# A graph network on one core: leaner lists in the first stage, two scalar products merged, and the needs of the third pass's gathers found one aggregate sooner

## The reference, cut to what matters

```python
# first layer: three passes
for l in range(3):
    neigh = segment_sum(h[src], dst) * inv_deg
    h = h @ Ws_self[l] + neigh @ Ws_neigh[l] + bs[l]      # relu after passes 0 and 1
x = layernorm(x + h)
# second layer, called with idx_i = src, idx_j = dst: messages of an edge
s, v = hs[idx_j], hv[idx_j]                               # 32 scalars, 32 x 3 vectors
Wf = (ssp(f_ij @ W1 + b1) @ W2 + b2) * rcut               # filters, four kinds are used
s*ys*Wf0, (v.yv)/sqrt(3)*Wf1, s*yv*Wf2, v*ys*Wf3          # summed per source node
x = layernorm(x + dense(sums))
```

## Time and profile before

| | us |
|---|---|
| median of 3 runs (lowest, highest) | 1964.1 (1961.87, 1965.44) |
| the profiled execution | 1961.11 |
| its span, first to last instruction | 1959.3 |
| mean granted TensorE clock | 0.985 |
| PE busy | 1863.8 (95%) |
| DVE busy | 1285.2 (66%) |
| POOL busy | 1075.7 (55%) |
| ACT busy | 591.9 (30%) |

### The profile page before, as it was taken

The page is one execution under the profiler, slowest core; times in us unless marked ns, Lnnn a source line. Parts: engine busy times, 40 slices in busy tenths (PEclk is TensorE's granted clock), DMA queues, the critical chain, the costliest instruction groups (busy, mean ns, idle before and its releaser), DMA issues. The chain is left out here.

```text
span 1959.3 us, 23685 instructions
## 1 busy us (share of the span) xinstructions
PE 1863.8 (95%) x8451; PEld 1191.1 (61%) x8451; DVE 1285.2 (66%) x1989; ACT 591.9 (30%) x1380; POOL 1075.7 (55%) x1018
## 2 busy tenths in 40 slices
PE   6799989999999999999999999999998988999996
PEld 3344445555555555555555555666665877888885
DVE  5899999869973334333333434555553988999997
ACT  1355542300000000000000000111113876888884
POOL 4000000000038878888887886188887777777773
PEclk9899999999999999999999999999998998999998
DMA  5145454322223323332332234455554344444441
GB/s 151 60 167 173 154 205 169 126 90 88 84 86 107 112 82 112 113 95 92 95 99 80 90 95 142 141 187 192 192 192 152 96 103 108 108 108 111 112 116 50
DMA packets 127305, 236.72 MB, mean 121 GB/s; under 512 B 28134, under 2 KB 70835, under 8 KB 127184
## 3 DMA queue, kind: packets, MB, share of 16 engines
q1 hardware_dynamic: 93152, 179.50, 28.6%
q0 software_dynamic: 34032, 55.66, 10.6%
HBM read 159.94 MB, written 75.11 MB: 120 GB/s over the span
## 5 line engine op out<-in xcount | busy, mean ns | idle before, releaser
L1115 PE MATMUL low<-table,abuf 125*125 125x512 f16 x3750 | 843.1, 380 | 4.8 <-DVE abuf L1554 4.8
L1115 PEld LDWEIGHTS low<-table,abuf 125*125 125x125 bf16 x3750 | 505.0, 137 | 300.0 <-issue 27.5
L957 PE MATMUL mid<-wbuf,h_t 128*125 128x512 f32 x1200 | 558.9, 602 | 6.1 <-DVE st_out L1601 4.5
L820 POOL DMA_INDIRECT by_src<-scat_row,sort x416 | 482.4, 1160 | 126.0 <-issue 118.5
L825 POOL DMA_INDIRECT table<-msg_table,wbuf x294 | 318.5, 1083 | 90.7 <-issue 81.3
L957 PEld LDWEIGHTS mid<-wbuf,h_t 128*125 128x125 f32 x1200 | 214.8, 190 | 210.3 <-issue 199.6
L812 POOL TENSOR_TENSOR scat_row<-scat_row 128x64 f32<-128x64 f32 x26 | 16.0, 615 | 524.3 <-DVE sort L1721 523.8
L1608 DVE SCALAR_TENSOR_TENSOR y<-low,inv_deg,st_in 125x512 f32<-125x512 f32 x75 | 56.2, 750 | 315.5 <-PE low L1115 198.4
L1554 DVE TENSOR_TENSOR abuf<-abuf,row_scale 125x3125 bf16<-125x3125 bf16 (+3 forms) x84 | 256.5, 3059 | 2.1 <-DMA abuf<-adj 2.0
L1149 PE MATMUL low<-table,wbuf 128*125 128x256 f32 x900 | 217.2, 392 | 31.2 <-DVE table L1851 30.7
L850 POOL DMA_INDIRECT sort<-msg_table,sort x156 | 193.0, 1237 | 82.3 <-issue 82.0
(11 more groups left out here) (215 smaller groups left out, 1636.3 us busy)
## 6 DMA issues: line engine op xcount, KB each, us to landing
abuf<-adj SPq DMA_DIRECT2D x75, 781.2 KB, 4.9
adj<-table SPq DMA_DIRECT2D x25, 781.2 KB, 4.6
states<-st_out SPq DMA_DIRECT2D x75, 256.0 KB, 2.0
st_in<-states SPq DMA_DIRECT2D x75, 256.0 KB, 4.9
early_rows<-sort POOLq DMA_DIRECT2D x30, 320.0 KB, 2.8
table<-early_rows SPq DMA_DIRECT2D x25, 384.0 KB, 6.5
by_src<-scat_row,sort POOLq DMA_INDIRECT x416
by_src<-blank SPq DMA_DIRECT2D x25, 252.0 KB, 4.0
```

What stands on the lines that cost most here:

```text
L820: pool.indirect_dma_start(out=by_src, out_offset=bass.IndirectOffsetOnAxis(ap=place_i[:, k * PIECE + j:k * PIECE + j + 1], axis=0), in_=sc ...
L957: last = pe.matmul(to[0:TN, :], h_t[i % 2][:, k, :], weights[l % 2][:, a, k, :], start=k == 0, stop=k == KC - 1)
L1115: last = pe.matmul(p_agg[k % 2][0:TN, :], a_tile[k % 3][:, a, :], table[ps % 2][0:TN, a, h, :], start=a == 0 and h == 0, stop=a == TILES - ...
```

## The change

- **First stage.** The degrees are counted by POOL (5 compares of 640 elements, then sums by halves), no longer by L1467 and L1469 on DVE. The codes are transposed in two parts, and the number of rounds needs only the first. The store and the load of the degrees move from SP's w = 4 to w = 12 and 13, their transpose and reciprocals to w = 14. PE waits for the rounds behind product 5, not ahead of it. Columns are kept as f32. `own_part` stands ahead of `row_lo`. The second block product moves by one step where it waited for ACT (`BLOCK_STEPS`). In `row_scales` the factor 4096 goes into the integer, so that L1566 is gone. The second tile of x is loaded ahead of the first layer's Ws. SP's small loads of constants are 3 per tile, not 2; W2 is loaded by columns in another order.
- **Third pass.** `early_max` at k = 53, transposes and `early_need` at k = 54. SECOND is 29: one step more ahead of the last stage, and one left over, which is spread from tile 8 on, not 3.
- **Last stage.** The products of the scalars with two filters (L1838 and L1843) become one of 384 elements; the order is `vy`, merged product, vector product, reduce. So ACT's `av` is ready later within a group.

```diff
-SECOND = GS * CHUNKS - 2
+SECOND = GS * CHUNKS - 1
+FILTERS_AT = (2 * F, 3 * F, 0), (0, 2 * F, F), (3 * F, 4 * F, 3 * F)
...
+    BLOCK_STEPS = (0, 1, 3, 4, 5, 6, 7)
...
+            load_x(1)
             load_weights(0, 1)
-            load_x(1)
...
-                    for to, of in later[(w - 8) * 2:(w - 7) * 2]:
+                    for to, of in later[(w - 8) * 3:(w - 7) * 3]:
...
-                if w == 4:
+                if w == 12:
                     sp.wait_ge(s_degn, 1)
                     sp.dma_start(bass.AP(degrees.tensor, 0, [[NODES, EP], [NODES * EP, GB], [1, NODES]]), node_deg[:, :, :]).then_inc(s_degst, 16)
+                if w == 13:
                     sp.wait_ge(s_degst, 16)
                     sp.dma_start(deg_row[:, :], degrees.rearrange("(t d) -> t d", d=TN)).then_inc(s_degld, 16)
...
             load_rows(0)
+            pool.wait_ge(s_codes, 1)
+            for d in range(NODES):
+                pool.tensor_scalar(in_node[:, :, d, :], part_d[:, :, 0:P], float(d), None, ALU.is_equal).then_inc(s_innode, 1)
+            half, step = P // 2, NODES
+            while half:
+                pool.wait_ge(s_innode, step)
+                step += 1
+                if half > 1:
+                    pool.tensor_tensor(in_node[:, :, :, 0:half], in_node[:, :, :, 0:half], in_node[:, :, :, half:2 * half], ALU.add).then_inc(s_innode, 1)
+                else:
+                    pool.tensor_tensor(node_deg[:, :, :], in_node[:, :, :, 0], in_node[:, :, :, 1], ALU.add).then_inc(s_degn, 1)
+                half //= 2
...
-                    n = (t - 3) * (NG - 1) + g - 1
+                    n = (t - 8) * (NG - 1) + g - 1
...
-                        pool.wait_ge(s_gd, 3 * (NG * (t - 2) + g) + 2)
+                        pool.wait_ge(s_gd, 3 * (NG * (t - 2) + g) + 3)
...
+                if w == LAG + 8:
+                    pe.wait_ge(s_degld, 16)
+                    pe.transpose(p_agg[1][0:TN, 0:TILES], deg_row[:, :], ident[0:TILES, 0:TILES]).then_inc(s_degt, 1)
...
+                product(w, 0, blocks_between)
+                if w == LAG - 1:
+                    codes_second()
+                product(w, 1, blocks_between)
+                if w == LAG - 2:
+                    codes_first()
                 if w == LAG - 1:
                     pe.wait_ge(s_meta, 1)
-                    pe.wait_ge(s_degld, 16)
-                    pe.transpose(p_b[1][0:TN, 0:TILES], deg_row[:, :], ident[0:TILES, 0:TILES]).then_inc(s_degt, 1)
                     general(pe, general_counts)
...
-                    if k == 55 and a == 4:
+                    if k == 54 and a == 4:
...
-                ch.link(dve.tensor_tensor(in_node[:, :, :, :], part_d[:, :, 0:P].unsqueeze(2).broadcast_to([EP, GB, NODES, P]),
-                                          node_iota32[0:EP, 0:NODES].unsqueeze(1).unsqueeze(3).broadcast_to([EP, GB, NODES, P]), ALU.is_equal))
-                dve.tensor_reduce(node_deg[:, :, :], in_node[:, :, :, :], AX.X, ALU.add).then_inc(s_degn, 1)
...
-                ch.link(dve.tensor_scalar(row_inv_i[0:TN, :], row_pow[0:TN, :], -1.0, float(254 << 23), ALU.mult, ALU.add))
-                dve.tensor_scalar(row_inv[0:TN, :], row_inv_i[0:TN, :].bitcast(F32), 4096.0, None, ALU.mult).then_inc(s_inv, 1)
+                dve.tensor_scalar(row_inv_i[0:TN, :], row_pow[0:TN, :], -1.0, float(266 << 23), ALU.mult, ALU.add).then_inc(s_inv, 1)
...
             for w in range(TILES):
                 if w == LAG - 1:
-                    degrees_and_rounds()
+                    rounds()
                     general(dve, general_counts)
-                    dve.wait_ge(s_cols, 4)
+                    dve.wait_ge(s_cols, 2)
...
                 row_scales(w)
+                own_part(w)
                 row_lo(w)
-                own_part(w)
...
+                if w == LAG + 8:
+                    mean_factors()
...
-                if k == 55:
+                if k == 54:
                     early_need()
...
-                if k == 54:
+                if k == 53:
                     early_max()
...
-                dve.tensor_tensor(av[n % 2][:, :, 0:F], s, w[:, :, 0, :], ALU.mult)
-                dve.tensor_tensor(av[n % 2][:, :, F:G].rearrange("p j (c f) -> p j c f", c=C3), v,
-                                  w[:, :, 3, :].unsqueeze(2).broadcast_to([P, GS, C3, F]), ALU.mult).then_inc(s_av, 1)
                 dve.tensor_tensor(vy[:, :, :, :], v, angle, ALU.mult).then_inc(s_gd, 1)
+                if n >= 2:
+                    dve.wait_ge(s_m, n - 1)
+                dve.tensor_tensor(products[:, :, 0:2 * F].rearrange("p j (k f) -> p j k f", k=2), s.unsqueeze(2).broadcast_to([P, GS, 2, F]),
+                                  w[:, :, W_AB:W_S + 1, :], ALU.mult).then_inc(s_gd, 1)
+                dve.tensor_tensor(products[:, :, 2 * F:F + G].rearrange("p j (c f) -> p j c f", c=C3), v,
+                                  w[:, :, W_V, :].unsqueeze(2).broadcast_to([P, GS, C3, F]), ALU.mult).then_inc(s_av, 1)
                 dve.wait_ge(s_m, n)
-                dve.tensor_tensor(ab[:, :, :], s, w[:, :, 2, :], ALU.mult).then_inc(s_gd, 1)
```

More of the change, by code:

```diff
@@ L29 @@
 KC = D // P
+W_AB, W_S, W_VY, W_V = range(4)
 B, F, R, YD, C3 = 128, 32, 20, 4, 3
@@ L156, in gnn_kernel @@
     place_i = sort.take(P, [CH], I32)
+    cols = Region(sort_sb[:, :], 7 * CH * 4)
+    cols.at = 4 * CH * 4
+    col_b = cols.take(P, [N // NODES])
+    col_c = cols.take(P, [(GB - 1) * EP])
+    col_last = sb("col_last", [P, EP])
     early = Region(sort_sb[:, :], 7 * CH * 4)
@@ L215, in gnn_kernel @@
     part_a = alias.take(EP, [GB, P])
[L216 to L219, removed]
+    part_b = alias.take(EP, [GB, P], at=5 * 4 * D + 4 * 6272)
+    part_c = alias.take(EP, [GB, P], at=5 * 4 * D + 4 * 6272 + 2560)
     alias.at = 5 * 4 * D
@@ L248, in gnn_kernel @@
     gfirst = pre.take(EP, [GB], I32)
+    in_node = pre.take(EP, [GB, NODES, P], BF16, at=4096)
+    node_deg = pre.take(EP, [GB, NODES], at=4096 + 6400)
     falls = oh_b[0].rearrange("p a d -> p (a d)")[0:EP, 0:EC]
@@ L267, in gnn_kernel @@
     msg_slots = [treg.take(P, [SLOTS, G]) for _ in range(2)]
-    av = [treg.take(P, [GS, G]) for _ in range(2)]
-    ab = treg.take(P, [GS, F])
+    av = [treg.take(P, [GS, F + G]) for _ in range(2)]
     vy = treg.take(P, [GS, C3 * F]).rearrange("p j (c f) -> p j c f", c=C3)
@@ L505, in gnn_kernel @@
         consts.append((b1_sb[F * j:F * j + F, :], b1.rearrange("(f a) -> f a", a=1)))
-        blocks.append((w2_sb[F * j:F * j + F, j, :], w2))
-        blocks.append((w2_sb[BLK * F:BLK * F + 1, j, :], b2.rearrange("(a f) -> a f", a=1)))
+        for lo, hi, at in FILTERS_AT:
+            blocks.append((w2_sb[F * j:F * j + F, j, at:at + hi - lo], w2[:, lo:hi]))
+            blocks.append((w2_sb[BLK * F:BLK * F + 1, j, at:at + hi - lo], b2[lo:hi].rearrange("(a f) -> a f", a=1)))
         blocks.append((w1_sb[PAY * j:PAY * j + R, F * j:F * j + F], w1))
@@ L992, in transpose_codes, with codes_second @@
                     pe.transpose(p_b[0][:, g * EP:(g + 1) * EP], part_b[:, g, :], ident[0:EP, 0:EP])
-                    last = pe.transpose(p_b[1][:, g * EP:(g + 1) * EP], part_c[:, g, :], ident[0:EP, 0:EP])
-                last.then_inc(s_ctp[0], 1)
+                    pe.transpose(p_b[1][:, g * EP:(g + 1) * EP], part_c[:, g, :], ident[0:EP, 0:EP])
+                pe.matmul(p_agg[0][0:1, 0:1], flags[0:EP, 2:3], ones32[0:EP, 0:1], start=True, stop=True).then_inc(s_ctp[0], 1)
+            def codes_second():
                 pe.wait_ge(s_cols, 2)
                 pe.transpose(p_b[0][:, 0:EP], part_b[:, GB - 1, :], ident[0:EP, 0:EP])
-                pe.transpose(p_b[0][:, P:P + EP], part_c[:, GB - 1, :], ident[0:EP, 0:EP])
-                pe.matmul(p_b[1][0:1, 0:1], flags[0:EP, 2:3], ones32[0:EP, 0:1], start=True, stop=True).then_inc(s_ctp[1], 1)
+                pe.transpose(p_b[0][:, P:P + EP], part_c[:, GB - 1, :], ident[0:EP, 0:EP]).then_inc(s_ctp[1], 1)
             def general_counts(q):
@@ L1061, in _, with blocks_between @@
                 tb = builder_of(w)
+                if w == LAG + 8:
+                    pe.wait_ge(s_degld, 16)
+                    pe.transpose(p_agg[1][0:TN, 0:TILES], deg_row[:, :], ident[0:TILES, 0:TILES]).then_inc(s_degt, 1)
+                def blocks_between(step):
+                    if tb is not None and step in BLOCK_STEPS:
+                        multiply_blocks(tb, BLOCK_STEPS.index(step))
+                product(w, 0, blocks_between)
[4 more added lines that the diff above has]
+                    codes_first()
                 if w == LAG - 1:
                     pe.wait_ge(s_meta, 1)
[L1064 to L1065 removed]
                     general(pe, general_counts)
[L1068 to L1075 removed]
             for k in range(AGGS):
@@ L1259, in _ @@
                     transposed(w + 1, ACT.Copy)
-                if w == LAG - 2:
-                    columns()
+                if w == LAG - 1:
```

(7 more changed lines are left out.)

101 lines of the change are left out of this document (55 added, 46 removed).

## The result

The changed kernel takes 1925.7 us (median of 4 runs, 1924.5 to 1933.2) beside 1963.0 of the kernel before in the same session: a ratio of 0.982, 95% interval 0.9803 to 0.9837, faster by some 35 us. 1927.0 and a range of 1914 to 1939 were forecast. The profiled execution took 1924.52 us (span 1922.6; 1961.11 and 1959.3 before), so 36.7 us of span are to be explained.

The account below looks back on a forecast made before the run. DVE bounds the first stage, PE the passes, POOL's gathers the last stage. From 1961.1 us, -27.2 (-12.7 - 15.0 + 0.5) and -9.7 (-1.9, -7.8) give 1924.2; with 3.0 for the median, 1927, range 1914 to 1939.

Parts of the forecast that it names:

- The tile, -0.79: First stage: without L1566 and with own_part in DVE's hole, each tile takes 9.37 us, 0.79 less; -15.0 over 19 tiles.
- The hole, -12.7: First stage, wait ahead of the first one-hot: it starts at 59.2 instead of 71.92, taken as -12.7 us.
- GpSimd's hold on VectorE, +0.5: First stage: POOL's count of degrees can hold up DVE's first one-hot, taken as 0.5 us.
- The bound of 6.9: First stage: the most that POOL's count of degrees could hold up DVE's first one-hot, 6.9 us.
- Third pass: Needs found sooner: POOL's first early gather comes 12.0 us sooner against the aggregates, the second list 3.7 us sooner.
- the start of the last stage, set at 1508.4: Last stage's start: POOL waits for the last message rows, L825 starts at 1508.4 instead of 1510.3, -1.9 us.
- Five gathers and a store less, -7.8: Last stage: five late gathers (6.9 us) and a store (0.9) drop out of POOL's work, -7.8 us.
- "POOL never pauses, so it sets the length.": Last stage: POOL's gathers follow without a pause at about 1.38 us each, so POOL decides how long it lasts.
- Rival C: Last stage: DVE takes over as bound, -17 us there and less by the merged product, 1918 us; chance 0.10.
- Merged product, 0: Last stage: one 384-element product saves DVE 0.07 us per group but av comes later; taken as 0, ends -5 and +2.
- E, the slow rival: Last stage: ACT scales 0.87 us later and DVE waits in all 75 groups, 65 us less 37, 1992 us; chance 0.03.

Follow-up runs that it names:

- experiment 5: The changed kernel without GpSimd's count of degrees, one memset writing 17 instead: 2042.8 us beside 2093.0 of the kernel before.
- experiment 1: The kernel before with only the 4096 folded into row_inv's integer and own_part put ahead of row_lo: 1947.9 us, ratio 0.992.
- experiment 3: The changed kernel with its third-pass part undone (needs at aggregates 54 and 55, SECOND lower by one, two late lists from tile 3): 1933.8 us, ratio 0.9849.
- experiments 1 to 4: Includes two more on the changed kernel: late gathers back at tile 3, 1928.3 us; last-stage group order put back, merged product kept, 1935.6 us.
- 8: The changed kernel with a third order in each last-stage group (merged, vector product, v times angles, product with angles, reduction, last product): 2015.2 us beside 2093.0.

## Why the prediction was right, and where it was not

- **The tile, -0.79.** It was 0.84, 9.32 us; alone it moved the first aggregate by -15.2 (forecast -15.0). Right, and shown by itself. ACT's gap in VectorE's tile is filled by `own_part`, and PE follows.
- **The hole, -12.7.** The first one-hot moved by 12.27 (59.65; 59.2 was worked out). These edits were not run by themselves; their worth is read from the trace.
- **GpSimd's hold on VectorE, +0.5.** Mis-sized: 2.55 by experiment 5. I had "VectorE mostly waits then"; in fact compares and sums last 27 us (53.35 to 80.6) and lie beside two tiles of one-hots. The bound of 6.9 held.
- **Forgotten**: `mean_factors`, which stays on VectorE, now in a tile that VectorE fills, costs 0.57 (the tile of 9.89 us in it). The stage gave 25.1 us at the first aggregate and 25.0 at the last mean, not 27.2.
- **Third pass.** First early gather 12 us sooner: right. The second list comes 1.1 us ahead of the last mean where it came 0.2 behind; the start of the last stage, set at 1508.4 for GpSimd, is not that engine's. Measured from the last mean, the first group came 1.0 later, not 1.9 sooner: PE's last message product (L993, 8 matmuls) took 1.89 us and not 1.16, and the row's store and SP's load wait for it. That is the clock: granted 0.50 in these 1.89 us, 0.85 in the 1.16 of before. Thirteen of the fourteen profiles have 1.88 or 1.89, that of experiment 1 among them, which leaves the third pass as it was; so it isn't the change.
- **Five gathers and a store less, -7.8.** The last stage behind its first group got 12.7 shorter. Undone (experiment 3), the third part costs 5.7 us by the timed ratios, 8.2 by medians, 12.8 by the profiled last stage, the place of the rest in them: the runs fit 7.8 and don't fix it. That such a gather costs its own length had a part missing: behind PE's stands in tiles 3 to 8 its clock was lower, and VectorE waited some 6 us for the slow sums.
- **"POOL never pauses, so it sets the length."** This step failed. The gathers fill the time in steady tiles because they are held up in step with VectorE, whose tile of 16.58 us is 12 x 1.38; the earlier trace rows had 228.7 of 232.7 us of VectorE beside it, and I passed over that. Only in tiles 3 to 8 was VectorE held up. Rival C had the mechanism (VectorE takes over) and too large a gain for it.
- **Merged product, 0.** Right in sum. What it saves (0.07 x 3 per tile) is waited for at the filters. E, the slow rival, had that wait in all 75 groups at 0.87 us; it is in one of three, at 0.32.

Total: -25.0 for -27.2 up to the last mean, +1.0 for -1.9 at the start of the last stage, -12.7 for -7.8 in it. The number was hit to 1.3 us because two misses to the one side, 2.2 and 2.9 us, and one of 4.9 to the other cancel: that is luck.

## What to carry to other kernels

An engine that shows no gap is the bound only if its neighbours have gaps: look at the busy share of every engine in the steady stretch, and be wary of a pitch that divides another engine's tile exactly. Work that can wait (here the late gathers) is best put where its engine has a lead, though the place alone was worth 0 to 4 us here. A stand costs more than itself where TensorE's clock falls behind it. In a stream of dependent vector instructions, put an independent one between a producer and its reader; it is worth more than a saved instruction start.

## What the runs showed of the hardware that I had not expected

- GpSimd is slow at this: a compare of 640 elements per partition takes 11.38/5 = 2.28 us, 3.6 ns per element, and the six sums, 25 x (64 + 32 + ... + 2) = 3150 elements, 15.47 us, 4.9 ns per element. VectorE did the same count in 3.5 + 3.5 us, so GpSimd's 27 us are nearly four times as long. By the 2.6 cycles per element against VectorE's one, which the page "GPSIMD Engine Reference" of the Trainium skill states (section Elementwise), less was to be expected; I had estimated 7 us for the sums from it, and the trace has 15.5.
- GpSimd holds VectorE only in part. The one-hot at 59.65 lies wholly beside compares and took 3.42 us, as without them; those beside the sums took 0.35, 0.52 and 1.49 us more. "SBUF — State Buffer" of the Trainium skill (section Who interferes with whom) has it that one engine blocks the other for a whole instruction; by that rule the first sum, half of the elements and so (an estimate) 7 to 8 us long, would have held the one-hot at 69.50 for some us, and the trace doesn't agree.
- A VectorE instruction that reads the output of the one right ahead starts 0.18 us later than an independent one.
- In the last stage PE's clock fell behind stands of 1.6 to 3.5 us: where sums behind the first tile are slow (4.2 to 5.5 us for twelve matmuls, not 2.8; the kernel before and experiments 1 to 4), PE had just waited that long. Not every such stand had it: at 1582.06 in experiment 1 one of 2.20 us was followed by sums of 2.85.
- On two of the chips the engines stood 3 us and more at a time, with times 6 to 7% higher for the kernel before and less for others (on the same chip 2043 us for experiment 5 and 2015 for 8, where the kernel before took 2093). Its cause stays open.
